# A four-slot ring of triangular Toeplitz tables, each fetched in three transfers, in the mixer loop of a sequence kernel

## What is computed

```python
xz = jnp.einsum('bld,ed->bel', hidden_states, W_in)      # 8 x 512 tokens of 128, 256 channels
x, z = jnp.split(xz, 2, axis=1)
x = silu(causal_conv_4_taps(x) + conv_b)
k = _s4d_kernel(log_dt, log_A_real, A_imag, C_re, C_im, L)   # one filter of 512 taps a channel
y = jnp.fft.irfft(jnp.fft.rfft(x, n=n) * jnp.fft.rfft(k, n=n), n=n)[..., :L]   # causal convolution
y = y + x * D[None, :, None]
y = y * jax.nn.silu(z)
return jnp.einsum('bhl,dh->bld', y, W_out)
```

## Time and profile before

| | |
|---|---|
| Median of 3 runs | 288.48 us (286.81 to 288.93) |
| The profiled execution: time, its span | 288.91 us, 287.2 us |
| PE busy, DVE, ACT, POOL | 86%, 60%, 65%, 44% of the span |
| First matmul of group 0, last matmul of the scan loop's tables (group 31) | 85.4 us, 141.1 us |
| POOL idle until L482, at 52.1 us, from | 5.1 us |
| Transfers to `TR` from `kernel_rows` | 32 of 512 KB, median 6.4 us from issue to landing |
| HBM read, written | 38.14 MB, 14.00 MB |

### The profile page before, as it was taken

The page is one execution under the profiler, slowest core; times in us unless marked ns, Lnnn a source line. Parts: engine busy times, 40 slices in busy tenths (PEclk is TensorE's granted clock), DMA queues, the critical chain, the costliest instruction groups (busy, mean ns, idle before and its releaser), DMA issues.

```text
span 287.2 us, 8709 instructions
## 1 busy us (share of the span) xinstructions
PE 245.9 (86%) x2801; PEld 217.6 (76%) x2801; DVE 171.1 (60%) x532; ACT 188.1 (65%) x522; POOL 125.7 (44%) x143
## 2 busy tenths in 40 slices
PE   4799999999957987999979999610999999999980
PEld 1688888888845655677769999500899999999970
DVE  2889985999354342455524565780066666676772
ACT  5879999846986664778746565200477777777740
POOL 5000000400049575999401777774004555544555
PEclk9999999999999797999999999955599999999996
DMA  6748977200399999998092321125367777677510
GB/s 215 213 111 343 346 291 279 118 0 0 118 289 332 282 316 275 248 317 229 3 346 96 96 86 57 51 60 188 97 191 212 213 206 215 195 203 208 173 37 5
DMA packets 54243, 52.12 MB, mean 181 GB/s; under 512 B 4399, under 2 KB 42801, under 8 KB 54082
## 3 DMA queue, kind: packets, MB, share of 16 engines
q1 hardware_dynamic: 50930, 45.60, 52.8%
q0 software_dynamic: 2272, 4.27, 4.3%
q10 hardware_dynamic: 1008, 1.84, 1.9%
HBM read 38.14 MB, written 14.00 MB: 182 GB/s over the span
## 4 chain that ended last, share of the span: by engine, by line
PE 82%; POOL 5%; issue 5%; DMA 2%; DVE 2%; ACT 2%; SPq 0%; DVEq 0%; ACTq 0%; POOLq 0%
PE banks L1155 20%; PE banks L1321 13%; PE banks L1332 11%; PE banks L1207 6%; PE banks L1158 5%; PE banks L1273 5%; POOL dispatched_rows L529 4%; PE banks L1217 4%; PE banks L1200 4%; PE banks L1221 4%; PE banks L1256 2%; PE banks L1271 2%; PE banks L1311 2%; PE banks L1290 1%; PE banks L1165 1%
## 5 line engine op out<-in xcount | busy, mean ns | idle before, releaser
L1155 PE MATMUL banks<-Wx,XT 128*128 128x256 f32 x256 | 62.4, 388 | 1.4 <-DVE Wx L785 1.4
L544 POOL DMA_INDIRECT out<-X x39 | 38.3, 982 | 49.3 <-DVE X L1111 40.5
L737 ACT ACTIVATE Z<-banks,BR 128x128 f32<-128x128 f32 x156 | 44.7, 367 | 20.4 <-PE banks L1321 20.2
L1155 PEld LDWEIGHTS banks<-Wx,XT 128*128 128x128 f32 x256 | 49.6, 195 | 10.1 <-DVE Wx L785 3.0
L476 POOL TENSOR_TENSOR Wx<-BR,RE 128x384 f32 (+1 forms) x32 | 47.9, 1524 | 8.8 <-PE banks L1200 8.8
L1321 PE MATMUL banks<-Z 128*128 128x128 f32 x312 | 43.4, 285 | 0.0
L529 POOL DMA_INDIRECT dispatched_rows<-TR,CR x32 | 31.3, 977 | 23.1 <-issue 22.1
L1332 PE MATMUL banks<-BR,Z 128*128 x312 | 40.9, 275 | 0.0
L1321 PEld LDWEIGHTS banks<-Z 128*128 128x128 f32 x312 | 40.0, 201 | 0.1
L1332 PEld LDWEIGHTS banks<-BR,Z 128*128 128x128 f32 x312 | 37.8, 192 | 0.0
L966 DVE TENSOR_TENSOR X<-banks,Z 128x256 f32 (+1 forms) x32 | 13.6, 425 | 26.9 <-PE banks L1221 26.8
(11 more groups left out here) (195 smaller groups left out, 463.0 us busy)
## 6 DMA issues: line engine op xcount, KB each, us to landing
TR<-kernel_rows SPq DMA_DIRECT2D x32, 512.0 KB, 6.4
Z<-w SPq DMA_DIRECT2D x35, 256.0 KB, 2.9
dispatched_rows<-TR SPq DMA_DIRECT2D x3, 2310.0 KB, 8.8
X<-dispatched_rows SPq DMA_DIRECT2D x39, 66.0 KB, 2.7
XT<-hidden_t SPq DMA_DIRECT2D x10, 256.0 KB, 3.3
RE<-decay_and_turns SPq DMA_DIRECT2D x2, 1024.0 KB, 7.3
BR<-w SPq DMA_DIRECT2D x1, 2048.0 KB, 8.1
dispatched_rows<-TR SPq DMA_DIRECT2D x1, 1848.0 KB, 7.9
```

What stands on the lines that cost most here:

```text
L544: pool.indirect_dma_start(out_rows, bass.IndirectOffsetOnAxis(XS[:, n % ROWS_RING, TOKEN_COL:TOKEN_COL + 1].bitcast(U32), 0), F[:, slot, : ...
L737: last = nc.scalar.activation(HT[:, slot, c * P:c * P + P], bank[n % 4][:, c * P:c * P + P], ACT.Relu, bias=B1[:, bass.ds(experts[n % 4] * ...
L1155: mm(bank[X_BANKS[k]][:, j * CHAN:(j + 1) * CHAN], XT[:, slot, at:at + CHUNK], Wx[:, tap, :], start=(tap == 0), stop=(tap == TAPS - 1))
```

## The change

The ring has 4 slots, at columns 2048 to 6143 of `TR`, which no longer overlap `Sel`, `empties` and the moved `Kx`. `TR` itself shrinks to 8192 columns, so the loop bodies of PE and of SP hold 4 groups and run seven times (`GROUPS // T_SLOTS` turns, the first written out). Each table comes in three transfers: partitions 0 to 31 with all 128 columns, 32 to 63 with 96, 64 to 127 with 64. What they leave out is zero in the matrix; POOL writes those zeros into all four slots once, and SP waits for it before the first load. The semaphore of a slot rises by 48 a turn.

```diff
+T_PARTS = ((0, 32, CHUNK), (32, 64, CHUNK - 32), (64, P, CHUNK - 64))
-T_SLOTS = 8
+T_SLOTS = 4
+TR_COLS = 8192
-    toeplitz = bass.AP(kext.tensor, 0, [[1, P], [KROW, CHAN], [1, CHUNK]])
+    toeplitz = [bass.AP(kext.tensor, low, [[1, high - low], [KROW, CHAN], [1, CHUNK]]) for low, high, _ in T_PARTS]
-        TR = sb("TR", [P, T_SLOTS * GH * CHUNK])
+        TR = sb("TR", [P, TR_COLS])
-        Tring = TR[:, :].rearrange("p (s h u) -> p s h u", s=T_SLOTS, h=GH)
+        Tring = TR[:, 2048:2048 + T_SLOTS * GH * CHUNK].rearrange("p (s h u) -> p s h u", s=T_SLOTS, h=GH)
-        Kx = TR[:, 4096:4096 + 2 * KROW].rearrange("p (j c) -> p j c", j=2)
+        Kx = TR[:, 6400:6400 + 2 * KROW].rearrange("p (j c) -> p j c", j=2)
...
-                sp.dma_start(Tring[:, k, :, :], toeplitz[:, bass.ds(group * GH, GH), :]).then_inc(s_t[k], 16)
-
+                for (low, high, cols), part in zip(T_PARTS, toeplitz):
+                    sp.dma_start(Tring[low:high, k, :, 0:cols], part[:, bass.ds(group * GH, GH), 0:cols])\
+                      .then_inc(s_t[k], 16)
+
+            sp.wait_ge(s_tz, 2)
             for k in range(T_SLOTS):
                 load_toeplitz(0, k)
...
+            pool.wait_ge(s_const, 3)
+            for i, (low, high, cols) in enumerate(T_PARTS[1:]):
+                nc.gpsimd.memset(Tring[low:high, :, :, cols:], 0.0).then_inc(s_tz, 1)
+                pool.wait_ge(s_tz, i + 1)
...
-                pe.wait_ge(s_t[k], (r + 1) * 16)
+                pe.wait_ge(s_t[k], (r + 1) * 48)
```

More of the change, by code:

```diff
@@ L226, in build @@
         s_const = sem("constants_ready")
+        s_tz = sem("toeplitz_zeros_ready")
         s_pstep = sem("pool_step")
@@ L885, in _ @@
             dve.wait_ge(s_sel0, 1)
-            at = bass.AP(TR[:, :].tensor, 0, [[T_SLOTS * GH * CHUNK, P], [4 * 32, GROUPS // 4], [32 + GH, 4], [1, GH]])
+            at = bass.AP(TR[:, :].tensor, 0, [[TR_COLS, P], [4 * 32, GROUPS // 4], [32 + GH, 4], [1, GH]])
             tt(at, v(AMP).rearrange("p (a b) -> p a b", b=4).unsqueeze(3).to_broadcast([P, GROUPS // 4, 4, GH]),
```

## The result

The changed kernel takes 299.4 us (median of 4, 298.58 to 300.64) against 288.51 for the kernel before: ratio 1.0393, 95% interval [1.0333, 1.0452]. I had forecast 288.7, in a range of 282.8 to 293. It is slower by 11 us, and the profiled execution (300.64 us, span 298.9) shows SP's queue on the chain, as forecast, but at a higher price.

A forecast was written before the change was run, and what follows sets the result against it. PE held 82% of the chain; SP's queue would become the bound at 1.84 us a table, swallowing PE's 5.7 us gain: 288.9 + 0.2 = 289.1 us, for the median 288.7, range 282.8 to 293.

The forecast's parts named there:

- case A: Scan loop: SP's issues bound it at 1.77 to 1.93 us a table, 287.2 to 290.6 us; chance 0.53.
- Pace: SP's queue in the loop: three issues, gaps, threshold and loop end come to 1.84 us a table, against PE's 1.49.
- The bound I gave: SP's queue in the loop: 0.03 us more on each of the three issues gives 1.93 us a table.
- Start: SP's first load in the loop at 86.45; group 10's, due at 97.5, waits for group 6 and goes at 98.3.
- Landing: Loop's table loads: the last part, 128 KB in 512 runs, lands in 2.6 us, ends 1.9 and 3.8.
- The sign I had named: SP's loads: the forecast is wrong if an issue's length depends on its number of runs; no size given.
- B: SP's queue in the loop: parts share their register instructions, 1.73 us a table, 286.2 us; chance 0.12.
- C: Loop: PE stays the bound because short transfers hold SP under 0.27 us each, 282.8 us; chance 0.17.
- A's upper end: SP's queue in the loop: over 1.96 us a table, counted with D as slower by over 1%, together 0.23.
- D: 16 DMA engines: transfers with short runs become the bound, 294.4 us at r = 1.5, 307 at 2; chance 0.18.
- At nothing: Ahead of the loop: memsets (2.9 us of POOL), twelve first issues (5.8 us, done by 81.6), `Kx`'s new address cost nothing.
- PE's chain alone, -5.72: PE in the loop: groups 8 to 15 become repeats without late code, -5.72 us if nothing else holds it.

The follow-up runs named there:

- e2: The changed kernel with two transfers a table (partitions 0 to 63 whole, 64 to 127 with 64 columns): 288.4 us, ratio 1.003.
- e4: The changed kernel with the same 96 transfers and number of runs, each run a sixteenth as long: 299.2 us, ratio 1.039.
- e7: The changed kernel with one transfer a table, ring of 6, groups 0 and 1 written out, then a 6-group body run five times: 284.9 us, ratio 0.991.
- e8: The changed kernel with the same 96 transfers, each fetching only the first of the group's 8 channels: 294.1 us, ratio 1.027.
- e1: The changed kernel with one transfer a table of 128 partitions x 512 B, ring of 4, no zeros written: 286.2 us, ratio 0.996.
- e10: e7 with each table in two transfers of 64 partitions, all 128 columns: 297.5 us, ratio 1.026.
- e3: The changed kernel with SP's loads written out at constant addresses, without a hardware loop, same 96 transfers: 291.4 us, ratio 1.013.
- e5: The changed kernel with 128 instead of 96 columns in the second part: 299.0 us, ratio 1.043.
- e6: The kernel before, with only the split added: each 512 KB table in three transfers of 32, 32 and 64 partitions: 297.7 us, ratio 1.043.

## Why the prediction was wrong

The mechanism of case A was right: separate register instructions for each part, SP's queue as the bound from the first third of the loop on, PE's stalls gone and their 5.7 us swallowed. Its size was wrong. Group 31 was put at 140.7 us and came at 150.84. By the forecast's own terms:

- **Pace.** *"2 x 0.565 + 0.373 + 0.27 + 0.075 = 1.84 us a table."* The failed step is the length of an issue: I gave each of the three parts the 0.373 us that one transfer of a whole table held SP. The parts took 0.40, 0.32 and 0.61 us (+0.2 in a table), and a turn of the loop's end adds 0.10 instead of 0.075. Group 10's first issue to group 31's is 146.16 - 102.75 = 43.4 us, forecast 38.6: **+4.8**. The bound I gave, 0.03 us an issue, was too narrow.
- **Start.** *"Group 10's ... 98.3."* It went at 102.75: **+4.4**. 1.5 is the first load of the loop, 87.99 instead of 86.45. PE began its first table matmuls 1.05 us later than in the kernel before (86.69, 85.64), and they took 1.09 us instead of 0.62, for the granted clock stood at 0.5 (1.2 GHz) when the loop began, after the 3.2 us wait for ACT. Neither is shown to come from the change: the loops of all these kernels began at 85.6 to 87.4 us, and after the same wait the clock stayed full in the kernel before, e2, e4, e7 and e8. 2.6 are three issues of 1.08, 1.31 and 1.30 us and a gap of 0.63 us behind one of them. The pace over six tables adds 1.1; the wait of 0.8 for group 6 that was in the forecast falls away.
- **Landing.** From a table's first issue to its matmuls, 150.84 - 146.16 = 4.7 us instead of 3.73: **+0.9**. The last part begins 1.3 us after the first instead of 1.13 and lands in 3.35 us instead of 2.6. Its median in the loop is 3.2 us, in e4 with a sixteenth of the bytes 2.5, so 0.7 us of it hang on bytes.

The sum is 10.1 us. The other 1.3 us of the span (298.9 - 150.84 = 148.1 against 146.7) lie behind the loop; e1 has 146.8, e7 147.3, e4 147.5, so I count them as scatter, not as the change.

**The length of an issue.** The third part's 0.61 us are not merely the price of standing behind two others. These are the first table loads of the kernel before (128 partitions, 1024 runs), of e2 and of e10 (64 partitions, 512 runs), each on a queue that had issued nothing for 3 us:

```profile
75.83 0.38 SPq L395 DMA_DIRECT2D TR<-kernel_rows  x1
```

```profile
76.16 0.73 SPq L399 DMA_DIRECT2D TR<-kernel_rows  x1
```

```profile
75.97 0.74 SPq L399 DMA_DIRECT2D TR<-kernel_rows  x1
```

Half of the partitions held SP longer than all of them, and in e2's loop each part took 0.60 us. So a row of a transfer of another shape was the wrong source. The sign I had named, an issue that depends on its number of runs, came true in part: e8 takes the third issue from 0.61 to 0.48 us, but the 1024 runs of a whole table took less than either. Standing in a row counts as well: with gaps of 0.04 us the first two parts took 0.62 and 0.45 us (e3), and the second load of the kernel before took 0.58.

**The cases.** B is out: SP has 59 FUSED_REGOPS for 60 parts (the rows shown with e4), not a third of that. C was nowhere near; its condition, an issue under 0.27 us, comes to 0.255 by the forecast's own gaps, and A's upper end is 1.93, not the 1.96 of the chances, which changes nothing. D was given for another reason (short runs) and priced at 294; in e4 and e5 other lengths of run did not move the time, and the engines' share was 0.76 where it reached 1.24 in e6. "At nothing": the memsets (2.8 us of POOL from 5.1 us on) and the 12 first loads (7.0 us of SP instead of 5.8, done by 82.7) were covered, as said. PE's clock did fall once more: a wait of 1.51 us for a table ended at 102.93, and the granted clock was 0.72 over 102 to 108 us. It cost the loop nothing that the rows show, for SP's issues ran on at their gap of 0.27 us. By the Trainium skill, "Runtime: NRT & Kernel Launch", § Instruction fetch mechanics, each jump back could have stalled like a first pass. The trace does not bear that out: e7 jumps back four times and stalls once, in its first pass. What I called PE's chain alone, -5.72, measured -4.5 to -5.6 in e7.

**Open.** The three long issues begin at 91.01, 94.93 and 99.22 us, and the trace has packets of 16 KB on the core's instruction queue at 90.73, 94.76 and 99.06; in e4 the long ones begin at 90.24, 95.29 and 99.56 and the packets at 90.13, 95.21 and 99.05. e6 has five more such pairs, issues of 0.84 to 1.27 us that begin within 0.8 us of a packet. That a fetch of code holds up SP's issues is only a reading of this; no kernel tried it alone. Nor is it settled why a transfer over 64 partitions holds SP longer than one over 128, with 64 runs still 0.48 us.

## What to carry to other kernels

Before a transfer is split to save bytes, count the issues: here a table may cost its queue 1.49 us, one issue fits, three cost 2.07 and, with few runs or at constant addresses, still 1.91 and 1.78. Take an issue's length from a transfer of the same shape, in the same kind of row; that of a whole table said little about its parts. Keep transfers over all partitions, and shorten an unrolled hardware loop for its own sake: e7, with less code and a ring of six, gave 3 us without any change to the data.

## What the runs showed of the hardware

- A register-addressed issue costs SP its length plus about 0.18 us of register work before the next. The length hangs on the shape: 0.38 us for 128 partitions and 1024 runs on a quiet queue (kernel before), 0.60 to 0.74 for 64 partitions and 512 runs (e2, and the first of e10), 0.48 for 64 partitions and 64 runs (e8); a sixteenth of the bytes changed it by 1 ns at most (e4).
- Transfers over 32 or 64 partitions ran at 238 to 247 GB/s with an engines' share of 1.24, those over 128 at 341 to 345 with one of 1.14 (e6, e10; e1, kernel before).
- Where SP's queue is the bound, runs of 384 or of 512 B in the second part made no difference (299.4 us, and e5 299.0 with 32 KB more a table). What short runs cost the DMA engines no run here isolates.
- A loop body that has been run once came without a stall in every later turn, for bodies of 4, 6 and 8 groups (e1, e7, kernel before).
